# Mask reduction two subtiles ahead, layernorm statistics behind each accumulation, and layernorm, transpose and router tile by tile, in a masked-attention and LoRA-FFN kernel on eight cores

## The reference

```python
# attention: x is (16384 tokens, 4096); mask, weight are 4096 x 4096
bm  = mask.reshape(Nb, 32, Kb, 32).sum(axis=(1, 3)) > 0        # 128 x 128 blocks
w   = (weight.reshape(Nb, 32, Kb, 32) * bm[:, None, :, None]).reshape(N, K)
x   = layernorm(x + x @ w.T + bias)
# FFN with 8 low-rank experts, top 2 of them per token
logits = x @ Wr.T
topk_p, topk_i = top_k(softmax(logits), 2);  topk_p /= topk_p.sum(-1)
w_e = scatter(topk_p, topk_i)                                  # (tokens, 8)
h   = einsum('ti,eri->ter', x, A)                              # rank 16
out = x @ Wb.T + bias2 + einsum('ter,te,eor->to', h, w_e, Bm) * 2.0
x   = layernorm(x + out)
```

## Time and profile before

| | us |
|---|---|
| median of 2 runs (3396.74 and 3484.25) | 3440.5 |
| the profiled execution | 3395.8 |
| its span on the slowest core (core 7) | 3394.3 |
| spans of all cores | 3370.5 to 3394.3 |
| TensorE matmul busy | 2385.9 (70%) |
| VectorE busy | 1003.3 (30%) |
| ScalarE busy | 315.7 (9%) |

### The profile page before, as it was taken

One profiled execution on the slowest core, in us unless ns is written; L12 is line 12 of the kernel. 1 busy time (PEld: TensorE's weight loads), 2 busy tenths in 40 slices (PEclk: granted clock), 3 DMA queues, 4 the chain that ended last, 5 costly groups with the idle time before them and its releaser, 6 DMA issues.

```text
span 3394.3 us, 48632 instructions; the slowest of 8 cores (3370.5 to 3394.3 us)
## 1 busy us (share of the span) xinstructions
PE 2385.9 (70%) x21109; PEld 1932.7 (57%) x21109; DVE 1003.3 (30%) x1621; ACT 315.7 (9%) x256; POOL 90.6 (3%) x158
## 2 busy tenths in 40 slices
PE   2556565656462799999249999369999079949991
PEld 1445453535352577777138888258887068837881
DVE  1454535353536222222321111611111321151112
ACT  0000000000005000000430000400000610030005
POOL 2000000000000000000000000000000000000000
PEclk9767676768685899999669999679999589979995
DMA  9665656565640466766463333003331554513542
GB/s 112 115 118 107 114 112 113 113 113 114 111 90 1 76 139 140 152 131 137 121 165 103 86 94 103 26 26 92 89 103 52 161 160 134 154 52 84 147 129 99
DMA packets 264251, 363.96 MB, mean 107 GB/s; under 512 B 38626, under 2 KB 173794, under 8 KB 249570
## 3 DMA queue, kind: packets, MB, share of 16 engines
q0 software_dynamic: 50224, 119.63, 24.5%
q1 hardware_dynamic: 213818, 241.22, 23.9%
HBM read 377.69 MB, written 102.76 MB: 142 GB/s over the span
## 4 chain that ended last, share of the span: by engine, by line
PE 66%; DVE 17%; DMA 6%; issue 5%; ACT 5%; DVEq 0%; POOL 0%; ACTq 0%; SPq 0%; POOLq 0%
PE pmm L434 55%; DVE wstg L369 4%; DVE bs2t L317 4%; PE pT L391 4%; PE pmm L429 3%; DMA out<-outstg 3%; DVE bnb L583 3%; DVE wtb L404 3%; DMA xnat<-xin 1%; ACT L597 1%; DMA mstg<-mask 1%; PE pH L780 1%; ACT outstg L828 1%; ACT L828 1%; DMA wtb<-wts 1%
## 5 line engine op out<-in xcount | busy, mean ns | idle before, releaser
L434 PE MATMUL pmm<-wtb,x1t 128*128 128x256 bf16 x16384 | 1903.6, 275 | 0.0
L434 PEld LDWEIGHTS pmm<-wtb,x1t 128*128 128x128 bf16 x16384 | 1573.8, 99 | 250.4 <-issue 2.9
L452 DVE SCALAR_TENSOR_TENSOR xnat<-pmm,xnat 128x256 bf16<-128x256 f32 x512 | 217.6, 425 | 1834.7 <-PE pmm L434 921.6
L551 PE MATMUL pT<-ident,xnat 128*128 128x128 bf16 x1024 | 97.1, 261 | 348.3 <-DVE x1t L563 210.8
L391 PE MATMUL pT<-ident,wstg 128*128 128x128 bf16 x2048 | 192.3, 262 | 194.0 <-DVE wstg L369 165.8
L597 ACT ACT_TABLE_LOAD x32 | 41.1, 1283 | 2875.3 <-DVE vpe L590 2875.0
L551 PEld LDWEIGHTS pT<-ident,xnat 128*128 128x128 bf16 x1024 | 79.5, 118 | 366.5 <-issue 364.1
L391 PEld LDWEIGHTS pT<-ident,wstg 128*128 128x128 bf16 x2048 | 160.5, 118 | 223.0 <-issue 214.0
L404 DVE COPY wtb<-pT 128x1024 bf16<-128x1024 bf16 x256 | 170.6, 689 | 89.1 <-PE pT L391 87.5
L429 PE MATMUL pmm<-wtb,ones 1*128 1x256 bf16 x512 | 143.1, 279 | 56.8 <-DVE wtb L404 40.5
L583 DVE BATCH_NORM_STATS2 bnb<-xnat 128x6 f32<-128x512 bf16 x256 | 155.0, 679 | 1.0 <-DVE xnat L452 0.9
(11 more groups left out here) (60 smaller groups left out, 530.4 us busy)
## 6 DMA issues: line engine op xcount, KB each, us to landing
wts<-wtb SPq DMA_DIRECT2D x32, 2112.0 KB, 17.0
mstg<-mask POOLq DMA_DIRECT2D x32, 1024.0 KB, 11.1
wstg<-w POOLq DMA_DIRECT2D x32, 1024.0 KB, 10.3
wstg<-wb POOLq DMA_DIRECT2D x32, 1024.0 KB, 11.1
out<-outstg SPq DMA_DIRECT2D x64, 512.0 KB, 3.3
xnat<-xin POOLq DMA_DIRECT2D x16, 1024.0 KB, 12.0
wstg<-am POOLq DMA_DIRECT2D x1, 1024.0 KB, 10.2
wstg<-bm POOLq DMA_DIRECT2D x8, 128.0 KB, 10.7
```

The source lines that it names most:

```text
L434: mm = t.matmul(pmm[bk][:, 0:NCW], x1t[:, kt * maxchunk + i * 128: kt * maxchunk + (i + 1) * 128], wtb[sl][:, kt * NCW:(kt + 1) * NCW], st ...
L452: sV.inc(v.scalar_tensor_tensor(sl_ap, pmm[bk][:, 0:NCW], 1.0, sl_ap, ALU.mult, ALU.add))
L551: mm = t.transpose(pT[k][:, j * 128:(j + 1) * 128], xnat[:, i * D + kt * 128: i * D + (kt + 1) * 128], ident[:, :])
```

## The change

It has four parts.

- The mask part of `gen_subtile` becomes `maskpipe`. It is called for subtiles 0 and 1 at the start of the attention pass, and for subtile ntt + 2 ahead of `gen_subtile` for subtile ntt. Its result has a place for each of the 32 subtiles (`q2full`); there are still two `mstg` buffers.
- The layernorm statistics move from `ln_stats_apply` to `nci_matmuls`: one instruction of 256 columns behind each accumulation, with a wait on that accumulation, into `bnbt`, which holds 16 results of 6 numbers per tile. The aggregation reads 96 numbers in place of 48.
- Between attention and FFN each tile goes through layernorm, transposes (`transpose_tile`) and router before the next one starts.
- The router's exponential is taken of the logits without subtracting their maximum, directly behind their copy; the step that negates the maximum is gone.

```diff
+        q2_ready = [0] * KT
+
+        def maskpipe(ntt):
+            sl = ntt % 2
...
         def gen_subtile(L, ntt):
             sl = ntt % 2
-            if L == 0:
...
                 @block.vector
-                def _(v, ntt=ntt, sl=sl, gs=gs, gv=gv, q2_v=q2_v):
+                def _(v, ntt=ntt, sl=sl, gs=gs, gv=gv, q2v=q2_ready[ntt]):
                     v.wait_ge(gs.h, gv)
-                    v.wait_ge(sV.h, q2_v)
+                    v.wait_ge(sV.h, q2v)
...
-                state["bank_free"][bk] = sV.n
+                    v.wait_ge(sV.h, sV.n)
+                    sV.inc(v.bn_stats(
+                        bnbt[:, i * 96 + nci * 6:i * 96 + (nci + 1) * 6],
+                        sl_ap))
+                state["bank_free"][bk] = sV.n - 1
             state["wtb_free"][sl] = (sT, sT.n)
 
         def layer_pass(L, c, nt, lora):
+            if c == 0 and L == 0:
+                maskpipe(0)
+                maskpipe(1)
             for nci in range(NNC):
                 sl = nci % 2
                 if c == 0:
                     subs = []
                     for sub in range(2):
-                        ready = gen_subtile(L, nci * 2 + sub)
+                        ntt = nci * 2 + sub
+                        if L == 0 and ntt + 2 < KT:
+                            maskpipe(ntt + 2)
+                        ready = gen_subtile(L, ntt)
                         ev = gen_transposes(nci, sub, ready)
...
-                inst = None
-                for j in range(8):
-                    inst = v.bn_stats(bnb[iset][:, j * 6:(j + 1) * 6],
-                                      xnat[:, i * D + j * 512:
-                                           i * D + (j + 1) * 512])
-                sV.inc(inst)
-                v.wait_ge(sV.h, sV.n)
-                sV.inc(v.bn_aggr(mv[iset][:, :], bnb[iset][:, :]))
+                sV.inc(v.bn_aggr(mv[iset][:, :],
+                                 bnbt[:, i * 96:(i + 1) * 96]))
...
+            @block.scalar
+            def _(sc, iset=iset, cp_v=cp_v):
+                sc.wait_ge(sV.h, cp_v)
+                sC.inc(sc.activation(exr[iset][:, :], tlr[iset][:, :],
+                                     AF.Exp))
+            ex_v = sC.n
...
-            ln1_applies = []
             for i in range(nt):
                 ap = ln_stats_apply(i, i % 2, attn_done_v, None, False)
-                ln1_applies.append(ap[0])
-            transpose_block(nt, None, sC, ln1_applies)
-            x2t_done = state["x1t_ready"]
-            for i in range(nt):
-                router_tile(i, i % 2, x2t_done)
+                x2t_i = transpose_tile(i, [(sC, ap[0])])
+                router_tile(i, i % 2, x2t_i)
+            state["x1t_ready"] = sV.n
```

More of the change, by code:

```diff
@@ L529, in _ @@
                         g.wait_ge(xf[0].h, xf[1])
[L530 removed]
+                    in_gv[0] = gdma(
                         g, xnat[:, i * D:(i + 1) * D],
                         xin[t0 + i * 128:t0 + (i + 1) * 128, :])
[L533 to L569 removed]
+                transpose_tile(i, [in_gv[0]])
             state["x1t_ready"] = sV.n
@@ L661, in _ @@
             def _(v, iset=iset, tv=tv, rf=rf):
+                v.wait_ge(sT.h, tv)
+                if rf is not None:
+                    v.wait_ge(rf[0].h, rf[1])
+                sV.inc(v.tensor_copy(tlr[iset][:, :], pRE[:, 0:E]))
+            state["pre_free"] = sV.n
+            cp_v = sV.n
+            @block.scalar
[4 more added lines that the diff above has]
+            ex_v = sC.n
+            @block.vector
+            def _(v, iset=iset, ex_v=ex_v, cp_v=cp_v):
                 def stepv(inst):
```

185 lines of the change are left out of this document (80 added, 105 removed).

## The result

The changed kernel takes a median of 3414.2 us (43 executions); the kernel before takes 3399.5 us (42 executions), so the 3440.5 of two executions stood too high and its lower value, near the profiled execution, was the typical one. The ratio is 1.0043, with a 95% interval of 1.0028 to 1.0059: slower by 0.4%, some 15 us. The forecast was 3412 us, 15.8 more than the profiled execution of before. (Ratios leave lengthened executions out; where a median lies above what its ratio says, that is why.)

A forecast was written before the change was run, and what follows sets the result against it. TensorE bounds the multiply-only passes; elsewhere it waits on VectorE chains and hand-overs. 3.1 + 7.7 + 5.3 - 12.9 + 12.6 = +15.8 on 3395.8 makes 3412 us; 8-in-10 range 3385 to 3455.

The forecast's parts named there:

- Gain per seam: 0: First attention pass: the mask reduction stays between last accumulation and masking in VectorE's order, so 6.54 us stay per subtile.
- 15 seams x 0.51 = +7.7: First attention pass: statistics behind each block's last accumulation delay the mask reduction from 0.35 to 0.86 us, +7.7 us.
- 15 x 0.35 = +5.3: First FFN pass: statistics behind each block's last accumulation delay the copy from 0.51 to 0.86 us, +5.3 us.
- The start: Start of first attention pass: two mask chains move here (13.1 us), plus a wait for the third mask load, +3.1 us.
- Rival 4: First FFN pass: added rest at seams lowers TensorE's clock, 15 x 4.6 = 69 us, 3481 us in all; chance 6%.
- My point of decision: First FFN pass: the clock rival decides once the seam's granted clock drops below 1; it stays at 1.00 today.
- The chunk ends: Three chunk ends: the first tile's statistics leave the path, the aggregation of 96 numbers costs 0.2 more, -12.9 us.
- rival 3: Chunk ends: output DMAs set the length anyway, so the 12.9 us gain does not come; 3425 us, chance 8%.
- Between attention and FFN: Tiles run one after another at 18.2 us each, 109.9 for six against 104.9; +12.6 us over three chunks.
- Rival 1: Between attention and FFN: tiles overlap and ScalarE sets the pace, 120 us less than before, 3279 us; chance 4%.
- Rival 2: First attention pass: the mask chain hides behind the matmuls, 30 x 6.54 = 196 us less, 3216 us; chance 2%.
- The table loads: ScalarE between attention and FFN: a load already precedes every activation, so alternating functions adds none; otherwise 17 us longer.

The follow-up runs named there:

- late statistic: The changed kernel with the statistics of each block's last tile held until the next block's first accumulation, except at the end of a pass; ratio 0.9974 to the kernel before.
- the fastest one: Changed kernel with masks among matmuls, all tiles joint between attention and FFN, late statistic, 36 extra matmuls ahead of each masking wait; ratio 0.8945 to the kernel before.

## Why the prediction was right or wrong

**The total** came near, 3412 against 3414.2, but not by its steps alone. Two of them failed: "Gain per seam: 0" for the mask, and the statistics' "15 seams x 0.51 = +7.7" and "15 x 0.35 = +5.3". Both priced a change at a seam by its own length, and put at nothing what it does to the clock at which the next block starts. Measured one by one, the statistics cost 16.7 and 10.2 us, and the mask's pass was 9 us shorter than the moved chains explain. In the first attention pass the two errors have opposite signs, and that the sum came out near is in part luck. Set against the 3440.5 of two executions the forecast would be a gain of 0.8%, and the change is a loss of 0.4%; against 42 executions the footing on the lower value was the right one. They also tell 0.4% from nothing (the interval is 1.0028 to 1.0059), where the prediction thought 2% the limit.

**The start** was right in kind: two chains and a wait, with the third mask landing 10.0 us after its issue. In size, +17.0 against +16.2 flatters it. Core 3's first block began at the high clock before and at the low one after (its first matmuls take 5.74 us with their bias, 4.07 before), which is 1.7 us of the 17.0. On cores 0, 1 and 2, which kept their level, the start grew by 13.3, 15.0 and 13.0. The two chains take 12.7 us rather than 13.1, and the wait is mostly shorter than 3.1.

**"Gain per seam: 0" for the mask** was right as to the chain and wrong as to the last row of it. Alone, the mask part gained 0.5%, and its pass was 9 us shorter than the two moved chains explain. What failed first was the assumption that a moved instruction keeps its waits: the masking now finds its input ready and starts 0.18 us earlier, twice a seam; the seams' lengths show 0.3 us of it each, some 4 us in all. The rest is the clock: three more of the first 14 seams are short ones, 7 us; the last seam has become one with a low clock, 2 us back.

**The statistics at the seams** were mis-sized. The length was right to 0.01 us (0.87 against 0.86). The price was not: alone, 16.7 for 7.7 in the attention pass, 10.2 for 5.3 in the FFN pass. The step "15 seams x 0.51" counted the delay alone, and each delay also changes how many blocks start at the low clock. In the attention pass of the whole change the mask's unforeseen gain and this unforeseen loss met: three short seams remain of 14 where there were five. So the -4.7 against -5.4 is in part luck; on cores 0 to 2, 4 and 5 the pass fell by 5.2 to 9.8. In the FFN pass nothing came against it: +10.7.

**Rival 4**, the clock in the FFN pass, came in part. I had it as all or nothing, with 69 us; it took three of 15 seams (three or four on every core). They are 13.1, 13.1 and 13.5 us long, the others 11.4 to 11.8. One that held and the stretch behind one that tipped, core 3 after, view of stretches:

```profile
1185.20:1191.00 5.80, 4.50 (x42) 3.69 (x42) 1.27 (x2) 0.00 (x0) 1.03 (x2) 1.00 0.97 197
...
1249.20:1255.00 5.80, 5.80 (x36) 4.17 (x37) 0.07 (x1) 0.00 (x0) 0.49 (x1) 0.71 1.03 207
```

The last transposes of the seam that tipped and the first matmuls behind it, in order of time:

```profile
1246.76 1.21 PE L396 MATMUL pT<-ident,wstg 128*128 128x128 bf16 x16 [0.41 <-DVE wtb L409]
...
1249.38 5.33 PE L439 MATMUL pmm<-wtb,x1t 128*128 128x256 bf16 x32
```

A tipped seam cost 1.7 us for its first matmuls (5.33 for the 3.67 of the earlier trace rows); the transposes, at 1.2 for 16, kept the high clock, so the 2.6 I had added for them did not come. 15 x 0.35 and 3 x 1.7 make 10.4 of the 10.7. My point of decision, a granted clock of the seam below 1, was in the wrong place too: the seam itself stays at 1.00, and the fall comes right behind it. Statistics issued twice tip six, the late statistic none. Of the prediction's signs of being wrong this is the one that came: a clock below 1.00 in the first FFN pass (0.99).

**The chunk ends** were right: -16.0 in all against -12.9 (with the statistics alone -16.6), and rival 3 (no gain there) is out.

**Between attention and FFN** the forecast was right in its chain (17.8 to 17.9 us a tile for 18.2) and in its sum (+13.1 against +12.6). Rival 1 is out, for the reason given: the order of VectorE's list. Batched again, the same three other parts give 0.9861; that shows the order tile by tile to be what cost the change its gain.

**Rival 2**, 3216 us with the mask chain hidden, did not come with this change, but the price was sound: once the reductions really stood among the matmuls, the kernel took 3227 to 3234 us.

**The table loads** came as forecast: 16 for 16 exponentials after as before, and the order in which the functions alternate added none.

So a large change moved the time little because its parts cancel. By their ratios exponential, mask and statistics gain 36, 17 and 9 us alone and 47 together, and the order tile by tile, put on top of them, costs 62: +15. (Alone on the kernel before it costs 109, since each tile's eight statistics of 512 columns then stand in its chain as well: 24.4 us a tile for 17.8.) The 36, 17 and 9 do not add up to the 47; their intervals are 12 to 16 us to each side, and the seams' clock makes the parts depend on each other.

## What to carry to other kernels

On engines that work in order, work is ahead of time only if it stands ahead of a wait in the list of the engine that does it: look for where its instruction stands, not for which tile it belongs to. In the stage that hands tiles through several engines it paid here to bring all tiles to each hand-over, not one tile to all of them. (Tile by tile with the next tile's first steps written ahead of this tile's router was not tried.) And where an engine's clock falls at rest, the few instructions that follow the last one of a block can carry all the cost of their kind, as 30 of 512 statistics did here: keep them behind the seam, and count a delay there with what it does to the block that follows.

## What the runs showed that I had not expected

- A delay of half a microsecond at a seam of 38 decides at which clock TensorE starts the next block, and it does so in a countable way: of the first 14 seams of the attention pass on core 3, five began at the high clock before, one with the statistics alone, three in the whole change, eight with the mask alone and eight with the late statistic. The counts hold from core to core, with the cores left out that had a stretch between the levels in that pass:

| kernel | of the first 14 blocks behind a seam of the attention pass, start at the high clock | of 15 seams of the FFN pass, followed by a low clock |
|---|---|---|
| before | 4 or 5 | 0 or 1 |
| mask alone | 7 or 8 | 1 |
| statistics alone | 0 or 1 | 3 |
| whole change | 3 or 4 | 3 or 4 |
| statistics twice | 0 or 1 | 6 |
| late statistic | 8 | 0 |

  What rule of rest and work decides a single block was not tried.
- In the changed kernel's profiled execution cores 6 and 7 had a stretch at a clock between the two levels. Core 7, view of stretches:

```profile
336.00:345.00 9.00, 9.00 (x68) 6.88 (x66) 1.66 (x4) 0.00 (x0) 0.00 (x0) 0.81 0.88 208
391.00:399.00 8.00, 8.00 (x72) 6.63 (x70) 1.71 (x4) 0.00 (x0) 0.00 (x0) 1.00 0.96 204
```

  There 32 matmuls took 4.38 us in place of 3.67. Cores 4 and 5 had such a stretch later, in the FFN pass of the second chunk, while cores 6 and 7 had not. The same view of core 5, and behind it of core 6:

```profile
2520.00:2630.00 110.00, 110.00 (x802) 84.12 (x801) 19.81 (x47) 0.00 (x0) 0.00 (x0) 0.81 0.29 80
...
2520.00:2630.00 110.00, 110.00 (x957) 90.89 (x955) 23.99 (x58) 0.00 (x0) 0.00 (x0) 1.00 0.27 77
```

  The Trainium skill, "TensorE: Matmul & The Clock Gate", section "Seeing it yourself", knows such a third state, at 13 of 16 pulses, and says that it takes the whole die while three of its cores multiply. The 0.81 agrees; that the whole die is taken does not, since core 4 of the same die kept 3.67 us while cores 6 and 7 were at 0.81. Here it came to two neighbouring cores at nearly the same time: 4 and 5, 6 and 7 in this execution, 0 and 1 with the late statistic (from 1176 and 1171 us), 4 and 5 with the extra matmuls in the changed kernel (both from 1149 us). What brings it on was not tried.
- Extra matmuls that nobody reads made a pass shorter: 42 us in the changed kernel, 34 us in the fastest one, with TensorE busier by 180 and 72 us.
